# Cross-attention sums turned by DMA in f16 parts instead of by TensorE in float32

## The reference

```
x = x + attention(layernorm(x))                    # self-attention, one head
x = x + xattn(layernorm(x), context)               # below
x = x + ffn_on_31_chosen_rows(layernorm(x))        # router, attention of 16 heads, feed-forward

def xattn(x, context):                             # 16 heads of 64, Nc = 1601 keys
    q = heads(x @ Wq); k = heads(context @ Wk); v = heads(context @ Wv)
    attn = softmax(q @ k.T * 64 ** -0.5)
    return (attn @ v).joined() @ Wo + bo
```

## Time and profile before

| | before |
|---|---|
| median of 3 runs | 2166.11 us (2165.36 to 2169.33) |
| span of the profiled execution | 2169.9 us |
| PE busy | 2103.3 us, 97% |
| POOL busy | 1933.6 us, 89% |
| ACT busy | 1832.2 us, 84% |
| DVE busy | 1736.7 us, 80% |
| PE's clock | full (0.9 or more) in every slice |
| DMA | 22.10 MB, mean 10 GB/s, mostly in the opening |

### The profile page before, as it was taken

How to read it: one execution, slowest core, us unless ns; L and a number is a source line. 1 busy time by engine, 2 the same in 40 slices (tenths; PEclk the granted TensorE clock), 3 DMA queues, 4 the chain that set the end, 5 groups by cost and what they waited for, 6 DMA issues and landing times.

```text
span 2169.9 us, 58374 instructions
## 1 busy us (share of the span) xinstructions
PE 2103.3 (97%) x22087; PEld 1544.3 (71%) x22087; DVE 1736.7 (80%) x4158; ACT 1832.2 (84%) x3124; POOL 1933.6 (89%) x1127
## 2 busy tenths in 40 slices
PE   8999999999999999999999999999999999999998
PEld 4677777777777777777777777777777777777665
DVE  7778878787887888879687797878878788886764
ACT  6898898989888888998888888898878888888872
POOL 3899999999999899999899998998989999899991
PEclk9999999999999999999999999999999999999999
DMA  3110000000000000000000000000000000000000
GB/s 73 42 38 13 2 13 2 2 13 2 13 2 2 13 2 13 2 13 2 11 13 2 13 2 2 14 2 13 2 11 13 2 13 2 2 2 2 2 11 11
DMA packets 17366, 22.10 MB, mean 10 GB/s; under 512 B 5872, under 2 KB 14976, under 8 KB 17088
## 3 DMA queue, kind: packets, MB, share of 16 engines
q1 hardware_dynamic: 15984, 18.17, 3.0%
q10 hardware_dynamic: 1104, 0.20, 0.1%
HBM read 16.14 MB, written 2.10 MB: 8 GB/s over the span
## 4 chain that ended last, share of the span: by engine, by line
PE 76%; DVE 11%; issue 5%; ACT 5%; POOL 2%; DMA 0%; SPq 0%; DVEq 0%; ACTq 0%; POOLq 0%
PE PS L573 14%; PE PS L613 13%; PE PS L574 13%; PE PS L590 11%; PE PS L592 10%; PE PS L636 4%; DVE EH L1091 4%; PE PS L646 2%; PE PS L623 2%; DVE over L1114 2%; POOL EL L1566 2%; ACT PF L897 2%; PE PS L657 1%; ACT over L919 1%; DVE junk L1359 1%
## 5 line engine op out<-in xcount | busy, mean ns | idle before, releaser
L1566 POOL TENSOR_TENSOR EL<-PF,EH 124x1024 f16<-124x1024 f32 x828 | 1761.7, 2153 | 144.0 <-DVE EH L1091 69.4
L897 ACT ACTIVATE PF<-PS 124x512 f32<-124x512 f32 x1664 | 972.6, 602 | 203.7 <-PE PS L574 190.1
L590 PE MATMUL PS<-Ch,EH 123*128 123x97 f16 (+1 forms) x6656 | 765.8, 207 | 22.9 <-POOL EL L1566 22.2
L592 PE MATMUL PS<-Cl,EL 123*128 123x97 f16 (+1 forms) x6656 | 762.3, 207 | 0.0
L1091 DVE TENSOR_SCALAR_CACHE_REDUCE EH<-PF 124x1024 f16<-124x1024 f32 x621 | 746.1, 1209 | 18.1 <-ACT PF L897 16.9
L590 PEld LDWEIGHTS PS<-Ch,EH 123*128 123x128 f16 (+1 forms) x6656 | 609.1, 98 | 181.5 <-issue 62.7
L1114 DVE CUSTOM_DVE_ANT_1 over<-over,PS 128x806 f32<-128x806 f32 x512 | 506.6, 989 | 284.7 <-ACT over L919 142.8
L592 PEld LDWEIGHTS PS<-Cl,EL 123*128 123x128 f16 (+1 forms) x6656 | 597.8, 98 | 168.2 <-issue 1.9
L573 PE MATMUL PS<-AH,ChT 97*124 97x512 f16 x1664 | 646.6, 389 | 6.5 <-ACT PF L897 5.8
L574 PE MATMUL PS<-AL,ClT 96*124 96x512 f16 x1664 | 633.7, 381 | 0.0
L919 ACT ACTIVATE over<-PS 128x806 f32<-128x806 f32 x512 | 433.4, 846 | 28.6 <-PE PS L613 8.6
(11 more groups left out here) (248 smaller groups left out, 1766.9 us busy)
## 6 DMA issues: line engine op xcount, KB each, us to landing
Cf<-in_ctx SPq DMA_DIRECT2D x16, 546.0 KB
X<-in_x SPq DMA_DIRECT2D x16, 128.0 KB, 2.4
out_x<-X SPq DMA_DIRECT2D x16, 128.0 KB, 1.7
msk<-in_attention_mask SPq DMA_DIRECT2D x4, 256.0 KB, 4.3
AH<-mh SPq DMA_DIRECT2D x63, 2.0 KB
Cf<-in_ctx SPq DMA_DIRECT2D x16, 53.6 KB
xWqT<-in_xWqT SPq DMA_DIRECT2D x2, 256.0 KB, 6.5
xWo<-in_xWo SPq DMA_DIRECT2D x2, 256.0 KB, 4.3
```

What stands on the lines that cost most here:

```text
L590: pe.matmul(PS[:, 6, u0:u0 + DC + 1], EH[0:kr, r, qs], Ch[j][0:kr, t, :], start=(t == 0 and q == 0), stop=False, skip_group_check=True)
L592: m = pe.matmul(PS[:, 6, u0:u0 + DC + 1], EL[0:kr, r, qs], Cl[j][0:kr, t, :], start=False, stop=(t == KT - 1), skip_group_check=True)
L897: act.activation(PF[:, n % PRING, :], PS[0:KP, 4 + n % 2, :], ACT.Exp).then_inc(sg("ex"), 1)
L1566: pool.tensor_tensor(EL[:, r - 1:r + 1, :], PF[:, f - 1:f + 1, :], EH[:, r - 1:r + 1, :], ALU.subtract).then_inc(sg("lo_pool"), 1)
```

## The change

The sums are divided and multiplied by DVE straight out of PSUM (`norm`), into Un in float32. Their f16 parts lie in UHL: the high part is made by ACT (`u_split`, times -KEEP, one for each pair); the low part is made by two DMAs a quad: SP copies the high part over the low part (`u_copy`), and POOL issues a DMA that reads Un in float32 and adds it to the f16 low part (`u_low`). SP then issues one DMA that transposes both parts at once into UT (`turn_u`: 12 blocks of 128x128 f16). M is scaled by a power of two and split into f16 parts MH and ML once, in the first sequence (`m_max`, `mtop`, `msplit`). `proj` is twelve f16 matmuls, high by high and low by low; the scales are undone when DVE adds to X. The copies to U, the transposes on PE, ACT's evictions and POOL's multiplication are gone. The steps after a quad's end are placed 1 (`u_split`), 2 (`u_copy`), 5 (`u_low`), 9 (`turn_u`) and 18 (`proj`) tiles later. The first three `av` of a pair now come together, one tile later than the two did. SP gets a list of its own, with `c_scat` six tiles later. `sel_rank` uses tensor_scalar forms that write an accumulator. M now shares the memory of KX.

```
+SPLIT_LATER, COPY_LATER, LOW_LATER, TURN_LATER, PROJ_LATER = 1, 2, 5, 9, 18
...
-        if late >= 1 and late % KT == 1:
+        if late >= 2 and late % KT == 2:
+            put(n, "av", late - 2)
             put(n, "av", late - 1)
-        if late >= 0 and late % KT:
+        if late >= 0 and late % KT >= 2:
             put(n, "av", late)
+        if late >= 0 and late % KT == KT - 1 and late // KT < B * HP - 1:
+            put(n, "norm", late // KT)
...
-                ("turn_u", B - 1, QD - 1, 0): 4, ("proj", B - 1, QD - 1): 1, ("sel_row", B - 1): 17,
+                ("proj", B - 1, QD - 1): 24, ("sel_row", B - 1): 17,
...
                     if t == 0 and n > 0:
-                        w.wait_ge(sg("u"), b * HP + hp)
+                        w.wait_ge(sg("un"), b * HP + hp)
...
+                    w.wait_ge(sg("ut"), 16 * i)
+                    kb = bank_free(s)
+                    w.wait_ge(sg("m_lo"), 1)
+                    for t in range(T):
                         for c in range(QC):
+                            for part, of in enumerate((MH, ML)):
+                                m = pe.matmul(PS[:, kb, t * D:(t + 1) * D], UT[:, (part * T + t) * QC + c, :],
+                                              of[:, qd * QC + c, :], start=(c == 0 and part == 0),
+                                              stop=(c == QC - 1 and part == 1))
...
+                elif k == "u_split":
...
+                    w.wait_ge(sg("un"), x + 1)
+                    w.wait_ge(sg("ut"), 16 * max(0, b * QD + qd - 1))
+                    hs = slice(2 * (x % 2), 2 * (x % 2) + 2)
+                    act.activation(UHL[qd % 2][:, 0, :, hs, :], Un[qd % 2][:, :, hs, :], ACT.Copy,
+                                   scale=-KEEP).then_inc(sg("uh"), 1)
+                elif k == "msplit":
+                    w.wait_ge(sg("m_scale"), 1)
+                    act.activation(M[:, :, :], M[:, :, :], ACT.Copy, scale=mscale[:, 0:1]).then_inc(sg("m_scaled"), 1)
+                    w.wait_ge(sg("m_scaled"), 1)
+                    act.activation(MH[:, :, :], M[:, :, :], ACT.Copy, scale=-REST).then_inc(sg("m_hi"), 1)
...
+                elif k == "norm":
                     x, = s.a
                     sums = PS[:, 6, 0:4 * (DC + 1)].rearrange("p (q c) -> p q c", c=DC + 1)
+                    w.wait_ge(sg("av"), (x + 1) * KT)
+                    dve.reciprocal(rden_u[:, x % 2, :], sums[:, :, DC]).then_inc(sg("u_r"), 1)
+                    w.wait_ge(sg("u_r"), x + 1)
+                    b, qd = x // HP, x % HP // 2
+                    w.wait_ge(sg("ul"), 16 * max(0, b * QD + qd - 1))
                     dve.tensor_tensor(
+                        Un[qd % 2][:, :, 2 * (x % 2):2 * (x % 2) + 2, :].rearrange("p t h c -> p h t c"),
...
-                    dve.tensor_tensor_reduce(out=rank[:, j, :], in0=cnt[:, j, 0, :], in1=cnt[:, j, 2, :], scale=1.0,
-                                             scalar=0.0, op0=ALU.add, op1=ALU.add, accum_out=spill())
-                    dve.tensor_scalar(keep[:, j, :], cnt[:, j, 1, :], NSEL + 0.5, None,
-                                      ALU.is_gt).then_inc(*own_step())
+                    for t in range(T):
+                        dve.tensor_scalar(rank[:, j, t:t + 1], cnt[:, j, 0, t:t + 1], cnt[:, j, 2, t:t + 1], None,
+                                          ALU.add, ALU.add, accum_out=spill())
+                    dve.tensor_scalar(keep[:, j, :], cnt[:, j, 1, :], NSEL + 0.5, None, ALU.is_gt, ALU.add,
+                                      accum_out=spill()).then_inc(*own_step())
...
+                elif k == "u_low":
+                    b, qd = s.a
+                    w.wait_ge(sg("un"), b * HP + 2 * qd + 2)
+                    w.wait_ge(sg("u_copied"), 16 * i)
+                    pool.dma_start(UHL[qd % 2][:, 1, :, :, :].rearrange("p t h c -> p (t h c)"),
+                                   Un[qd % 2][:, :, :, :].rearrange("p t h c -> p (t h c)"),
+                                   accum_op=ALU.add).then_inc(sg("ul"), 16)
...
-            for s in order:
+            for s in orders["sp"]:
...
+                elif k == "u_copy":
+                    b, qd = s.a
+                    w.wait_ge(sg("uh"), b * HP + 2 * qd + 2)
+                    w.wait_ge(sg("ut"), 16 * max(0, i - 2))
+                    high, low = (UHL[qd % 2][:, part, :, :, :].rearrange("p t h c -> p (t h c)") for part in range(2))
+                    sp.dma_start(low, high).then_inc(sg("u_copied"), 16)
+                elif k == "turn_u":
+                    b, qd = s.a
+                    w.wait_ge(sg("ul"), 16 * i)
+                    w.wait_ge(sg("pj_mm"), b * QD + qd)
+                    sp.dma_start(UT[:, :, :], UHL[qd % 2][:, :, :, :, :].rearrange("p w t h c -> p (w t h c)"),
+                                 transpose=True).then_inc(sg("ut"), 16)
```

More of the change, by code:

```diff
@@ L216, in put @@
         stream.append((n + shift.get(kind, 0), len(stream), (kind, *a)))
-    out += opening(engine)
+    out += opening("pe" if engine == "sp" else engine)
     groups, todo = beside_plan(), []
@@ L239, in whole_order @@
         done = n - AV_LAG - (KT - 1)
-        if done >= 2 and (done - 2) % KT == 0:
-            put(n, "norm", (done - 2) // KT)
-        for late, step in ((-2, ("turn_u", 0)), (2, ("turn_u", 1)), (5, ("proj",))):
-            late += KT
-            if done >= late and (done - late) % (2 * KT) == KT:
-                quad = (done - late) // (2 * KT)
-                put(n, step[0], quad // QD, quad % QD, *step[1:])
+        if done >= 0 and done % KT == SPLIT_LATER:
+            put(n, "u_split", done // KT)
+        for later, kind in ((COPY_LATER, "u_copy"), (LOW_LATER, "u_low"), (TURN_LATER, "turn_u"), (PROJ_LATER, "proj")):
+            since = done - KT - later
+            if since >= 0 and since % (2 * KT) == 0:
+                quad = since // (2 * KT)
+                put(n, kind, quad // QD, quad % QD)
     out += [step for _, _, step in sorted(stream)]
-    out += [("norm", B * HP - 1), ("turn_u", B - 1, QD - 1, 0), ("turn_u", B - 1, QD - 1, 1), ("proj", B - 1, QD - 1)]
+    out += [("norm", B * HP - 1), ("u_split", B * HP - 1), ("u_copy", B - 1, QD - 1), ("u_low", B - 1, QD - 1), ("turn_u", B - 1, QD - 1), ("proj", B - 1, QD - 1)]
     out += [("ln_stats2", B - 1), ("sel_w", B - 1), ("sel_row", B - 1)]
@@ L373, in build @@
         G = sb("G", [P, 2, H, DC], F16)
-        M = sb("M", [P, MC, D])
+        M = KX[:, :, :, :].rearrange("p b h k -> p (b h k)")[:, 0:MC * D].rearrange("p (c d) -> p c d", d=D)
+        MH = sb("MH", [P, MC, D], F16)
+        ML = sb("ML", [P, MC, D], F16)
+        mmx = sb("mmx", [P, 1])
+        mtop = sb("mtop", [P, 1])
+        mscale = sb("mscale", [P, 1])
+        mback = sb("mback", [P, 1])
+        pback = sb("pback", [P, 2])
         rden_u = sb("rden_u", [P, 2, 4])
@@ L395, in build @@
         qscale = sb("qscale", [P, 2, 4, 2])
-        U = [sb(f"U{i}", [P, 4, DC + 1]) for i in range(2)]
         Un = [sb(f"Un{i}", [P, T, 4, DC]) for i in range(2)]
-        UT = sb("UT", [P, T, QC, P])
+        UHL = [sb(f"UHL{i}", [P, 2, T, 4, DC], F16) for i in range(2)]
+        UT = sb("UT", [P, 2 * T * QC, P], F16)
         pmax = sb("pmax", [P, 2, H * T])
@@ L462, in build @@
         order = whole_order("pe")
-        orders = {e: whole_order(e) for e in ("act", "dve", "pool")}
+        orders = {e: whole_order(e) for e in ("act", "dve", "pool", "sp")}
         at = {(s.kind, *s.a): s.i for s in order}
@@ L669, in tensor_program @@
                                  ident[0:KP, 0:KP]).then_inc(sg("sg_mm"), 1)
+                elif k == "mtop":
+                    w.wait_ge(sg("mmx"), 1)
+                    kb = bank_free(s)
+                    pe.transpose(PS[:, kb, 0:P], mmx[:, :].to_broadcast([P, P]), ident[:, :]).then_inc(sg("mt_mm"), 1)
                 elif k == "gtop":
@@ L1151, in vector_program @@
                 elif k == "proj":
                     b, qd = s.a
+                    back = pback[:, b % 2:b % 2 + 1]
+                    if qd == 0:
+                        w.wait_ge(sg("m_back"), 1)
+                        w.wait_ge(sg("sigma"), b + 1)
+                        if b >= 2:
+                            w.wait_ge(sg("pj_x"), at["proj", b - 2, QD - 1])
+                        dve.tensor_scalar(back, u_scale[:, b % 4:b % 4 + 1], mback[:, 0:1], None, ALU.mult, ALU.add,
+                                          accum_out=spill()).then_inc(sg("pj_back"), 1)
@@ L1155, in vector_program @@
                     w.wait_ge(sg("pj_x"), i - 1)
-                    dve.tensor_tensor(X[:, T * b:T * b + T, :], PS[:, bank_of(s), 0:T * D].rearrange("p (t d) -> p t d", d=D),
-                                      X[:, T * b:T * b + T, :], ALU.add).then_inc(sg("pj_x"), 1)
+                    dve.scalar_tensor_tensor(out=X[:, T * b:T * b + T, :],
+                                             in0=PS[:, bank_of(s), 0:T * D].rearrange("p (t d) -> p t d", d=D),
```

(2 more changed lines are left out.)

110 lines of the change are left out of this document (34 added, 76 removed).

## The result

The changed kernel takes 2186.59 us (median of 4 runs, 2185.97 to 2188.84), the kernel before 2167.72 (4 runs, 2165.36 to 2169.65): ratio 1.0088, 95% interval 1.0074 to 1.0102. It is 19 us slower; the forecast was 51 us faster. The profiled execution after spans 2184.7 us, before 2169.9.

What follows compares the result with a forecast made beforehand. TensorE was taken to set the pace, POOL close behind. Matmuls -93, boundary +19, ACT's and POOL's waits +10, M +3, tail +10 gave -51 us from the median 2166.11: 2115 us, range 2082 to 2205.

Steps and rivals of the forecast that it cites:

- An edit that takes matmul time out pays nearly in full: TensorE's transposes and projection: 1.46 us less a quad, 93 us in all, nearly all gained since PE sets the pace.
- The later sums: A pair's first sums, one tile later: 1.7 to 2.3 us of other PE work first, covering DVE's lateness.
- The boundary: Between pairs, PE's wait until DVE frees the sums' bank: 0.15 us times 128, 19 us (0 to 77).
- It fits, with almost no room: POOL's queue: multiplications gone, 64 DMA issues of 1.1 us added, 120.3 us in a stage of 127.2, 94.6%.
- The rival in which POOL sets the pace: Whole stream: with issues of 2.15 us POOL, not PE, sets the stage's length; 2147 us, chance 0.18.
- an estimate of 64 us on top: POOL's adding-DMA issues: locked out by VectorE's two-port mode under the skill's rule, up to 1 us a quad.
- Transfers: From POOL's place to the projection: adding DMA 3.5 us, transposing 4.5, path 9.7 of 15.9 us, so hidden.
- The rival of late transfers: Before the projection: transfers come late and PE waits, slower than before; 2211 us at 17.4 us of path, chance 0.20.
- a forecast of +10: The tail, where nothing hides the new path: 14.6 us in place of 4.1, +10 us (8 to 22).
- M, +3 us (0 to 8): First stage: scaling and splitting M puts two passes each on ACT and DVE, beside PE's work.
- DVE and ACT: Their work: ACT net -76 us, only slack; DVE +71 for multiplying, -34 for rank and keep steps.
- the third, that waits take what the matmuls give: Stream: boundary waits and ACT's and POOL's waits at their far ends, 2213 us, or half, 2164; chance 0.10.

Runs made afterwards that it cites:

- b_less_pe: The kernel before with two thirds of TensorE's transposes of the sums and of the projection's products left out, nothing else changed: 2144.5 us.
- b_early_norm: The kernel before with VectorE dividing and multiplying the sums out of PSUM, ahead of its round, sums in the old order: 25 us above before.
- a_no_add: The changed kernel without its 64 adding DMAs, so the low part of the sums is left out: 17 us faster by the medians.
- b_less_all: The kernel before with TensorE's transposes and products and ScalarE's evictions cut to a third, GpSimd's multiplication to a quarter: 2122.14 us against 2167.11.

## Why the prediction was wrong, point by point

**"An edit that takes matmul time out pays nearly in full": this step failed.** It was read from PE's 97% and from its small waits for POOL. The size of the saving was right: the twelve products in a row take 0.68 us against an estimate of 0.65, and the stream's matmuls fell by 74 us against 81 for fourteen of sixteen sequences. Its price was not. `b_less_pe` gives 24 us for 85. The busy share says that PE was nearly always at work; it doesn't say that the others had room at the places where PE would now be early. They had 5 to 18% in the fullest stage, and, as the waits say, less than PE needed at places 3, 6 and 7.

**The later sums: this step failed too.** I counted the moved tile as 1.7 to 2.3 us of work that covers DVE's lateness, and its cost as nothing. It does cover it: in the kernel after, the sums' weight loads wait 7.4 us for DVE's product in all, where they wait 22.5 in `b_early_norm`. But the cover is made of scores that ACT must first make room for, and of products for the maxima that wait for DVE's `fold`, 11.3 us at place 3 in the kernel after. The move costs 34 us by itself, 4 to 6 on top of the division on the kernel before, and 19 in the changed kernel. The rule I should have drawn from the earlier trace rows: where ACT waits 190 us for PE in one place, PE may still outrun it in another.

**The boundary, 19 us (0 to 77).** The division on VectorE with the old order costs 25 us net of what ACT and POOL lost by it; with the later sums the two cost 29.

**The account.** Before to division 24.8, the later sums 6.1, the rest of the change -11.4: 19.5 us by medians, where the result has 18.9, since the runs of before had medians of 2167.1 to 2169.4. The last term is, between the profiled executions, -25 in the stream (1854.9 to 1829.7; the 74 us of matmuls less, 49 of waits more) and +16 outside it, mostly in the first sequence and the tail. I had -93 for that stream term alone. Put the two parts in the other order and they are 34 and -5; the sum is the same.

**POOL.** Its issue was set at 1.1 us; the row has 0.88, and from one low part to the next with an issue between them the starts are 0.65 us further apart in the shortest cases. Its busy time fell by 50 us against 42. "It fits, with almost no room" was right for its length, yet 8 us of the stream hang on these issues (`a_no_add`), since a queue that is 93% full (123.11 of 133) is late at places. The rival in which POOL sets the pace had the right engine and a wrong form: POOL is one of several, worth 7 us alone, 18 with PE lighter. The rule of the Trainium skill (SBUF — State Buffer, section SBUF: two separate sides) that GpSimd can't write descriptors while VectorE runs in a mode that uses both ports, an estimate of 64 us on top, did not show: the issues take 838 to 1073 ns, with no tail of long ones. Whether VectorE was in such a mode beside one of them no run here shows, so the rule is neither borne out nor refuted.

**Transfers.** They were hidden as forecast, and landed 3.5 and 3.7 us after their issue began, where the sum had 3.5 and 4.5 with the issue on top. In the tail, where nothing covers them, the chain of the kernel after has them one by one:

```profile
2133.46 0.57 DVE Un L1132
2134.05 0.53 ACT UHL L917
2134.60 2.14 DMA UHL<-UHL
2136.79 0.49 issue
2137.28 3.48 DMA UHL<-Un
2140.77 3.63 DMA UT<-UHL
2144.40 0.05 issue
2144.45 1.46 PE PS L642 x12
```

The adding one takes 3.5 us and the transposing one 3.6, each with its issue, where the prediction had 4.6 and 5.1. The Trainium skill's formula (DMA: Bandwidth & Descriptors, Anatomy of one DMA), which it gives for DMAs that GpSimd issues, gives an estimated 2.9 us for each, and these rows are 0.6 and 0.7 above it. The prediction says that the sum would be the same by it; that holds for the stream, but its tail would have come out 2.2 us shorter. Its 2.0 us for the copy in the tail had no row behind it; the copy took 2.1. The rival of late transfers didn't come. In the tail, from the division to the end of the addition it is 13.0 us against 3.9 before: +9.1, with a forecast of +10. Here the products take 1.46 us and not 0.68: the 24 matmuls without use end at 2138.4 and the granted clock then falls to the lower of its two levels, 1.2 GHz: 0.66 in the mean of 2140 to 2150.

**M, +3 us (0 to 8).** The first sequence is 6.2 us longer. ACT's two passes take 1.58 and 1.48 us, DVE's 1.75 and 2.63 (the latter after 1.8 us of waiting for ACT), and the granted clock, 1.00 before, is 0.66 in 100 to 110 us after gaps of PE there.

```profile
100.00:110.00 10.00, 8.64 (x59) 6.72 (x60) 5.85 (x11) 5.33 (x10) 4.95 (x5) 0.66 0.22 41
```

**DVE and ACT.** DVE gained 45 us of busy time (forecast 37), ACT lost 47 (forecast 76). The forecast added up durations, and so taken ACT lost 71 us, with a split of 527 ns in place of 480; the busy time counts instructions that overlap only once. The keep step is rid of its lock as forecast, 2166 ns to 148, but a part of it seems to have moved on: the next steps on X rose from 348 to 841 ns in the mean, 32 of them, which takes back 16 of some 30 us. One of them ran from 241.66 to 243.08 beside a POOL pass that ended at 242.92.

```profile
L1389 DVE TENSOR_SCALAR_CACHE_REDUCE keep<-cnt x16: 146/148/151, 241.1 to 2154.0; 128x2 f32<-128x2 f32 x16
...
L1400 DVE SCALAR_TENSOR_TENSOR X<-X,keep x32: 339/358/1420, 241.7 to 2154.8; 128x128 f32<-128x128 f32 x32
```

**The rivals.** The measured time lies in the third, that waits take what the matmuls give (2164 to 2213, chance 0.10). It named waits for DVE and of POOL; the largest one, of scores for exponentials after the moved sums, it did not. The range held the time only through the nearer parts of this rival and of late transfers.

**What stays open.** Of the 85 us taken from PE in `b_less_all`, 40 don't come back. The waits say where (places 3, 6 and 7), and in the changed kernel the earlier projection halved the waits of the queries (18.1 to 9.8 us), but no run moved them in `b_less_all`: that these places are the cause there is read from the waits, not shown. Why the maxima's products wait for `fold` only where the later sums and the division meet is not shown either; both steps stand in DVE's queue around place 3, and no run moved `fold`.

## What to carry to other kernels

Where an engine is 97% busy and three others over 80%, take a part of its work out of the old kernel and time that before pricing a change by it: here 85 us of matmuls were worth 24. In queues that run in order, what counts is which work stands ahead of each wait: the same twelve products one tile earlier or later were 22 us apart, and the division on VectorE first or last in its tile 91 us, 43 of them by way of TensorE's clock, which fell after the longer gaps. A move that gives an engine "other work first" isn't free if that work needs another engine's buffers; find the engine that must empty them and see what stands in its queue at that place.

## What the hardware showed that was not expected

- An accumulating DMA (f32 added into f16, 192 KB written) takes 3.5 us from GpSimd's issue to landing, a transposing one of 384 KB f16 3.7 us from SyncE's issue, of which the issue itself takes 1.45, over twice that of the 2 KB one (0.63).
- GpSimd's low parts are recorded 2211 ns long in the mean, where they were 2153, but the starts of two in a row are 2.095 us apart in both kernels, in the median. The longer records, 2.35 to 2.45 us, of which there are 181, have the same 2.095 us to the next start: they are no cost.
